# A pair of images moved in one DMA of 128 rows, in place of eight DMAs of sixteen

## The chip, the cores and the metric

One core of one Trainium2 chip runs the whole program. The metric is the time on the device in microseconds (us). A core has five engines with their own instruction streams: TensorE (PE), VectorE (DVE), ScalarE (ACT), GpSimd (POOL) and SyncE (SP). They meet at semaphores. DMAs are issued here from SP's and from ScalarE's stream, and all of them are carried out by the core's 16 DMA engines.

## The reference

Input x has the shape (32, 64, 56, 56) in float32. Two residual blocks follow each other, and each begins with a group norm of 32 groups, so of two channels each:

```
x = x + conv3x3(sign(gn(x)), sign(weight)) * scale            # 64 -> 64 channels, padding 1
r = relu(batchnorm(w_r @ gn(x) + b_r))                         # 64 -> 16 channels
ker = w_s @ r + b_s                                            # 16 -> 16 groups x 49 taps, per pixel
x = x + sum over the 7x7 taps of shifted gn(x) * ker           # an involution: the kernel differs by pixel
```

w_r and w_s are weight-normalised. The involution's 49 coefficients of a pixel are shared by the four channels of a group.

## The kernel before

Two images make a pair; there are 16 pairs. A pair fills 128 partitions: the 64 channels of one image and the 64 of the other, 56 x 56 values in each, so one partition's row is 12544 contiguous bytes, in SBUF as in DRAM. The tile xs holds three pairs (`xs[:, p % 3, :]`). The pair is loaded there, both residual blocks are added to it in place, and it is stored from there.

The first block is a convolution on TensorE (L512), added to xs by VectorE (L750). For the second block the normalised image is transposed by TensorE (L541), split into a high and a low half in float16 by ScalarE (`high`, L404) and VectorE (`low`, L783), and written to a scratch tensor in DRAM (`parts_out`, L270). From there SP reads it back as patches: two stacks of sixteen-row planes, `first_stack` (L287, eight DMAs) and `second_stack` (L295, two DMAs; ScalarE copies the rest of the second stack from the first, `copy_high`, L432). A pair has 7 slots of patches (E = 7) and each slot has 8 units, so 56 units. In a unit TensorE multiplies the patches by the span weights (L571), VectorE multiplies the result by relu's output (L792), GpSimd adds two halves (L365), and TensorE sums these for a slot (L589). The sums go to DRAM and come back rearranged (L424, L445, issued by ScalarE), are arranged (L454), transposed (L603) and added to xs (L804, `added`).

Each engine's order is written out by hand. While pair p runs through its 56 units, the preparation of pair p + 1 is put between them: row sums (L734) at units 0 to 3, convolution at units 11 to 17, transposes with their high and low halves at units 28 to 36, and the reduction with its relu (L552, L412) at units 37 and 38. The relu is copied to the partitions where VectorE needs it by sixteen small DMAs (`spread`, L305), which wait for it.

SP's order matters for this change. In slot s of pair p it issues the second stack of the next slot and the first stack of the one after that. Behind these it issues, in slot 2, the store of pair p - 1 (`store`, L262), once the last output of that pair is added; in slot 3, two parts of pair p + 1 and the load of pair p + 2 (`load`, L257), once pair p - 1 is stored; in slot 4, the other two parts and spread. SP works its list in order, so a wait or a DMA there stands in front of all the rest.

Both `load` and `store` go through ROWS16 (L23), a list of eight slices of sixteen partitions: 32 to 92 in steps of 4, 0 to 30 in steps of 2, 33 to 93 by 4, 96 to 126 by 2, 34 to 94 by 4, 1 to 31 by 2, 35 to 95 by 4, and 97 to 127 by 2. Each slice is one DMA of 16 rows x 12544 bytes, 196 KB. Readers wait for all eight: x_loaded and stored count 16 for each DMA, and XLOAD and STORE are 128.

Of the kernel before, what the change touches and what calls it, by code (L numbers as in the profile page):

```python
# [20 lines left out]
OTHER = [i ^ 1 for i in range(32)]  # L21
K, PAD = 7, 3
TAPS = K * K  # L23

ROWS16 = tuple(slice(*r) for i in range(2) for r in ((32 + 2 * i, 96, 4), (i, 32, 2), (33 + 2 * i, 96, 4), (96 + i, 128, 2)))

PY, PX = 4, 2
POS = PY * PX
# [36 lines left out]
P_N = P_CONV + 9 * C  # L65

FIRST_LOADS, LOADS, ZEROS = 16 * 2, 16 * 6, 4
XLOAD, STORE = 16 * 8, 16 * 8
FIRSTLOAD, SECONDLOAD = 16 * 8, 16 * 2
COPY = JY * 128  # L70
DWRITE = 16 * 2
# [36 lines left out]
def build(nc, x, consts, params, span, gb_all, out, pairs=PAIRS):  # L108
    xv = x.rearrange("(p b) c h w -> p (b c) (h w)", b=2)
    ov = out.rearrange("(p b) c h w -> p (b c) (h w)", b=2)  # L110
# [4 lines left out]
    with ExitStack() as ctx:  # L115
        def sb(name, shape, dt=F32):
            return ctx.enter_context(nc.sbuf_tensor(name, shape, dt))

        def sem(name):
            return ctx.enter_context(nc.semaphore(name))  # L120
# [6 lines left out]
        xs = sb("xs", [128, 3, HW])  # L127
# [44 lines left out]
        x_loaded = sem("x_loaded")  # L172
        stored = sem("stored")
# [79 lines left out]
        @block.sync  # L253
        def _(sp):
            def load(p):
                for rows in ROWS16:
                    sp.dma_start(xs[rows, p % 3, :], xv[p][rows]).then_inc(x_loaded, 16)  # L257

            def store(p):
                sp.wait_ge(out_added, 4 * (p + 1))  # L260
                for rows in ROWS16:
                    sp.dma_start(ov[p][rows], xs[rows, p % 3, :]).then_inc(stored, 16)  # L262

            def parts_out(p, k):

# [43 lines left out]
            sp.dma_start(t_par, params).then_inc(first_loaded, 16)  # L309
            sp.dma_start(mask[:], consts[:, C_M:C_N]).then_inc(first_loaded, 16)  # L310
            load(0)
            for dst, src in ((t_span, span), (t_gb, gb_all.broadcast_to((128, 2 * TAPS * GROUPS))),
                             (t_sel, consts[0:TAPS, C_SEL:C_E]), (ident[:], consts[:, C_ID:C_ID + 128]),
# [4 lines left out]
            if pairs > 1:  # L318
                load(1)
# [10 lines left out]
            for p in range(pairs):  # L330
                for s in range(E):
                    e = E * p + s
                    if e + 1 < EALL:
                        second_stack(e + 1)
                    if e + 2 < EALL:
                        first_stack(e + 2)
                    if p + 1 < pairs:
                        if s == 3:
                            parts_out(p + 1, 0)
                            parts_out(p + 1, 1)  # L340
                        if s == 4:
                            parts_out(p + 1, 2)
                            parts_out(p + 1, 3)
                            spread(p + 1)
                    if s == 2 and p > 0:
                        store(p - 1)
                    if s == 3 and p + 2 < pairs:
                        if p > 0:
                            sp.wait_ge(stored, STORE * p)
                        sp.wait_ge(x_loaded, XLOAD * (p + 2))  # L350
                        load(p + 2)
            store(pairs - 1)
            sp.wait_ge(stored, STORE * pairs)

# [560 lines left out]
```

## Time and profile before

| | |
|---|---|
| three timed runs | 1971.62 us median (1965.9 to 1975.86) |
| the profiled execution | 1978.51 us, span 1976.6 us |
| granted TensorE clock, mean | 0.922 |
| TensorE, busy | 1621.0 us, 82% |
| VectorE, busy | 1378.6 us, 70% |
| ScalarE, busy | 1052.8 us, 53% |
| GpSimd, busy | 1015.0 us, 51% |
| SP's DMA queue (q1) | 139728 packets, 356.81 MB, 74.2% of 16 engines' span |
| ScalarE's DMA queue (q10) | 75264 packets, 51.39 MB, 10.1% |

A row of the timeline names the start, the duration, the engine, the line of the program, the operation, the tile written and the tile read, and the count of instructions merged; in brackets stands how long the engine was idle before it and what ended that. SPq and ACTq are the streams that issue DMAs; the duration of such a row is the time of issuing, and the transfer itself lands later. A wait is put down to the releaser that came last.

### The profile page before, as it was taken

How to read it: one execution, taken by the hardware profiler on the slowest of the kernel's cores; microseconds unless marked ns; L12 is line 12 of the kernel's file. 1: busy time of each engine (PE TensorE's matmuls, PEld its weight loads, DVE VectorE, ACT ScalarE, POOL GpSimd, SP SyncE). 2: the span in 40 equal slices, each digit the busy share in tenths (PEclk: the TensorE clock that was granted, in tenths of full speed). 3: DMA queues.
4: the chain of work that ended last, by engine and by line, in shares of the span. 5: the costliest groups of instructions: out<-in, count | busy, mean ns of one | idle time of the engine just before them, and what ended most of it. 6: DMA issues, size and time to landing. Idle time of an engine off the chain costs nothing.

```text
span 1976.6 us, 39046 instructions
## 1 busy us (share of the span) xinstructions
PE 1621.0 (82%) x15072; PEld 730.2 (37%) x15072; DVE 1378.6 (70%) x1699; ACT 1052.8 (53%) x758; POOL 1015.0 (51%) x904
## 2 busy tenths in 40 slices
PE   3488897978889797896978878798887988889885
PEld 1233443434333343343433334333333433334332
DVE  5476776858768685776867767586776767768674
ACT  2255555545655554555545655465555545655562
POOL 1145555554645555455554645555455554645673
PEclk8799998999999998998989989898989999989997
DMA  4679899797998969899798998979799797998993
GB/s 106 158 168 237 185 238 224 199 233 172 245 216 217 236 173 239 186 244 215 188 240 181 250 215 205 230 183 247 175 240 225 187 250 180 248 215 205 227 243 85
DMA packets 215178, 410.70 MB, mean 208 GB/s; under 512 B 87406, under 2 KB 134815, under 8 KB 210847
## 3 DMA queue, kind: packets, MB, share of 16 engines
q1 hardware_dynamic: 139728, 356.81, 74.2%
q10 hardware_dynamic: 75264, 51.39, 10.1%
q8 instruction: 119, 1.95, 0.5%
q14 instruction: 67, 0.55, 0.1%
HBM read 310.30 MB, written 84.93 MB: 200 GB/s over the span
## 4 chain that ended last, share of the span: by engine, by line
POOL 46%; issue 42%; SPq 4%; DMA 2%; DVE 2%; PE 2%; ACT 1%; POOLq 1%; ACTq 0%; DVEq 0%
POOL folded L365 46%; SPq L305 2%; DMA patches<-parts_dram 1%; SPq L287 1%; PE ybank L571 1%; DMA back<-consts_dram 1%; POOLq L364 0%; SPq L257 0%; ACT patches L432 0%; DVE prod L792 0%; SPq L295 0%; PE ybank L541 0%; DMA parts_dram<-parts 0%; DVE parts L783 0%; SPq L270 0%
## 5 line engine op out<-in xcount | busy, mean ns | idle before, releaser
L365 POOL TENSOR_TENSOR folded<-prod 128x448 f32<-128x448 f32 x896 | 1009.3, 1139 | 941.3 <-DVE prod L792 940.0
L792 DVE TENSOR_TENSOR prod<-ybank,relu 128x896 f32<-128x896 f32 x896 | 961.1, 1088 | 406.9 <-PE ybank L571 333.4
L571 PE MATMUL ybank<-patches,wspan 128*64 128x448 f16 x7168 | 863.7, 382 | 240.2 <-DMA patches<-parts_dram 110.4
L432 ACT ACTIVATE patches<-patches 96x1792 f16<-96x1792 f16 x448 | 736.8, 1689 | 589.8 <-DMA patches<-parts_dram 306.9
L571 PEld LDWEIGHTS ybank<-patches,wspan 128*64 128x64 f16 x7168 | 396.3, 116 | 757.6 <-issue 416.1
L512 PE MATMUL ybank<-sgn,convw 128*128 128x448 bf16 x1008 | 205.6, 357 | 24.5 <-ACT sgn L385 20.1
L589 PE MATMUL obank<-folded,esum 128*32 128x448 f32 x1792 | 214.8, 551 | 1.5 <-POOL folded L365 1.5
L582 PE MATMUL obank<-patches,wbias 128*32 128x448 f16 x3584 | 197.8, 364 | 0.0
L512 PEld LDWEIGHTS ybank<-sgn,convw 128*128 128x128 bf16 x1008 | 93.4, 97 | 137.8 <-issue 33.5
L582 PEld LDWEIGHTS obank<-patches,wbias 128*32 128x32 f16 x3584 | 87.4, 99 | 105.2 <-issue 52.7
L783 DVE TENSOR_TENSOR parts<-ybank,parts 128x1024 f16<-128x1024 f32 x64 | 78.5, 1226 | 60.5 <-ACT parts L404 60.5
L750 DVE SCALAR_TENSOR_TENSOR xs<-ybank,scale,xs 128x896 f32<-128x896 f32 x64 | 66.0, 1032 | 73.7 <-PE ybank L512 73.6
L404 ACT ACTIVATE parts<-ybank 128x1024 f16<-128x1024 f32 x64 | 65.3, 1020 | 68.1 <-PE ybank L541 64.5
L603 PE MATMUL ybank<-back,blocks 128*128 128x128 f32 (+1 forms) x448 | 62.2, 284 | 44.2 <-DVE prod L792 36.0
L541 PE MATMUL ybank<-ident,xn 128*128 128x128 f32 x512 | 74.3, 293 | 20.9 <-DVE parts L783 20.1
L420 ACT ACTIVATE osb<-obank,alpha 128x448 f32<-128x448 f32 x112 | 69.3, 619 | 29.7 <-PE obank L589 29.7
L603 PEld LDWEIGHTS ybank<-back,blocks 128*128 128x128 f32 (+1 forms) x448 | 48.2, 153 | 77.7 <-DVE prod L792 52.2
L541 PEld LDWEIGHTS ybank<-ident,xn 128*128 128x128 f32 x512 | 59.4, 148 | 44.4 <-DVE parts L783 25.5
L454 ACT ACTIVATE blocks<-rows 128x1792 f32<-128x1792 f32 (+1 forms) x32 | 54.1, 1690 | 40.0 <-DMA relu<-blocks 31.9
L754 DVE BATCH_NORM_STATS2 bn<-xs 128x6 f32<-128x448 f32 x112 | 70.2, 627 | 3.9
L804 DVE TENSOR_TENSOR xs<-ybank,xs 128x1024 f32<-128x1024 f32 (+1 forms) x64 | 61.8, 966 | 12.8 <-PE ybank L603 12.7
L734 DVE TENSOR_REDUCE rowsums<-xs 128x14 f32<-128x784 f32 x64 | 61.1, 959 | 12.5 <-DMA xs<-x_dram 12.5
(90 smaller groups left out, 380.0 us busy)
## 6 DMA issues: line engine op xcount, KB each, us to landing
patches<-parts_dram SPq DMA_DIRECT2D x1120, 224.0 KB, 7.0
parts_dram<-parts SPq DMA_DIRECT2D x128, 256.0 KB, 7.7
xs<-x_dram SPq DMA_DIRECT2D x128, 196.0 KB, 5.0
sums_dram<-osb ACTq DMA_DIRECT2D x112, 224.0 KB, 6.2
rows<-sums_dram ACTq DMA_DIRECT2D x112, 224.0 KB, 6.6
out_dram<-xs SPq DMA_DIRECT2D x128, 196.0 KB, 3.7
relu<-blocks SPq DMA_DIRECT2D x256, 49.0 KB
patches<-gb_dram SPq DMA_DIRECT2D x1, 784.0 KB
```

The source lines that it names most:

```text
L365: pool.tensor_tensor(folded[:, u % 8, :], prod[:, u % 2, 0, :], prod[:, u % 2, 1, :], ALU.add).then_inc(fold_done, 1)
L420: act.activation(osb[:], Obank[e % 2][:, 0:N], ACT.Copy, scale=alpha[:]).then_inc(o_read, 1)
L432: act.activation(X2[0:COPIED_ROWS, e % 2, at], X1[0:COPIED_ROWS, e % 3, at], ACT.Copy).then_inc(copied, 1)
L512: mm = pe.matmul(bank("conv", p, k)[:, i, 0:CW], convw[:, tap, :], sgn[:, CR * row + dh:CR * row + dh + CR, dw:dw + W], start=(tap == 0), ...
L541: mm = pe.transpose(bank("t", p, k)[:, y, 128 * h:128 * h + 128], xn[:, COLS * cy:COLS * cy + COLS], ident[:])
L571: mm = pe.matmul(bank("unit", p, n)[64 * t:64 * t + 64, h, 0:N], wspan[:, stack, g, h, :], of_group(e, stack, g), start=(stack == 0), stop ...
L582: pe.matmul(Obank[e % 2][32 * t:32 * t + 32, 0:N], wbias[:, stack, g, :], of_group(e, stack, g), start=(stack == 0 and i == 0), stop=False)
L589: mm = pe.matmul(Obank[e % 2][32 * (gp // 2):32 * (gp // 2) + 32, 0:N], esum[:, 16 - 16 * (gp % 2):48 - 16 * (gp % 2)], folded[:, 4 * half ...
L603: mm = pe.transpose(bank("out", p, k)[:, i, rows * n:rows * (n + 1)], V[0:rows, by].rearrange("m b g c -> m (b g c)"), back[0:rows, group, ...
L754: link(dve.bn_stats(bn[:, row, :], at[:, i, :]))
L783: dve.tensor_tensor(at(1), bank("t", p, k)[:], at(0), ALU.subtract).then_inc(low_done, 1)
L792: dve.tensor_tensor(prod[:, u % 2].rearrange("m h (n c) -> m h n c", c=GC), bank("unit", p, n)[:, :, 0:N].rearrange("m h (n c) -> m h n c" ...
```

## The change

The load of a pair becomes one DMA over all 128 partitions, and so does the store. The list ROWS16 goes, and the counts that readers wait for fall from 16 x 8 to 16. Nothing else is touched: the order on SP, the tiles and the bytes moved are the same.

```
-ROWS16 = tuple(slice(*r) for i in range(2) for r in ((32 + 2 * i, 96, 4), (i, 32, 2), (33 + 2 * i, 96, 4), (96 + i, 128, 2)))
...
-XLOAD, STORE = 16 * 8, 16 * 8
+XLOAD, STORE = 16, 16
...
             def load(p):
-                for rows in ROWS16:
-                    sp.dma_start(xs[rows, p % 3, :], xv[p][rows]).then_inc(x_loaded, 16)
+                sp.dma_start(xs[:, p % 3, :], xv[p]).then_inc(x_loaded, 16)
 
             def store(p):
                 sp.wait_ge(out_added, 4 * (p + 1))
-                for rows in ROWS16:
-                    sp.dma_start(ov[p][rows], xs[rows, p % 3, :]).then_inc(stored, 16)
+                sp.dma_start(ov[p], xs[:, p % 3, :]).then_inc(stored, 16)
```

## Rows read from the trace of the kernel before

**Rows 1.** Waits of the engines: engine, line, waited for: us, times, longest.

```profile
PE ybank L571 <- DMA patches<-parts_dram: 110.4, 15, 9.1
...
ACT patches L432 <- DMA sums_dram<-osb: 68.3, 13, 7.4
...
PE ybank L541 <- DVE parts L783: 20.1, 10, 3.2
...
DVE scale L672 <- DMA back<-consts_dram: 5.6, 1, 5.6
```

**Rows 2.** Waits of SP's queue.

```profile
SPq L305 <- ACT blocks L412: 20.0, 9, 4.1
```

**Rows 3.** Timeline of SP's queue, one pair, 493 to 550 us.

```profile
493.85 5.97 SPq L262 DMA_DIRECT2D out_dram<-xs  x8
499.92 1.89 SPq L295 DMA_DIRECT2D patches<-parts_dram  x2
502.04 5.21 SPq L287 DMA_DIRECT2D patches<-parts_dram  x8
...
512.87 5.67 SPq L257 DMA_DIRECT2D xs<-x_dram  x8
...
525.24 2.79 SPq L270 DMA_DIRECT2D parts_dram<-parts  x4
529.05 13.36 SPq L305 DMA_DIRECT2D relu<-blocks  x16
```

**Rows 4.** Timeline of TensorE, the same pair.

```profile
496.93 0.95 PE L571 MATMUL ybank<-patches,wspan 128*64 128x448 f16 x8
...
519.83 1.09 PE L541 MATMUL ybank<-ident,xn 128*128 128x128 f32 x8 [2.09 <-DVE parts L783]
...
547.89 4.69 PE L571 MATMUL ybank<-patches,wspan 128*64 128x448 f16 x24 [8.33 <-DMA patches<-parts_dram]
```

**Rows 5.** Timeline of ScalarE, the same pair.

```profile
514.32 3.28 ACT L432 ACTIVATE patches<-patches 96x1792 f16<-96x1792 f16 x2 [4.01 <-DMA patches<-parts_dram]
517.51 1.00 ACT L404 ACTIVATE parts<-ybank 128x1024 f16<-128x1024 f32 x1
```

**Rows 6.** Stretches: engines' busy us, TensorE clock, DMA share, GB/s (last two).

```profile
4.00:11.50 7.50, 0.00 (x0) 0.00 (x0) 0.00 (x0) 1.35 (x2) 2.22 (x3) 1.00 0.98 214
11.90:13.30 1.40, 0.00 (x0) 0.00 (x0) 0.78 (x1) 0.00 (x0) 0.00 (x0) 1.00 0.97 383
...
518.60:529.00 10.40, 9.15 (x100) 3.24 (x104) 6.68 (x7) 6.77 (x6) 4.64 (x4) 1.00 1.01 220
```

**Rows 7.** DMA issues by line: count, size of one, median us to landing.

```profile
xs<-x_dram SPq DMA_DIRECT2D x128, 196.0 KB, 5.0
...
patches<-params_dram SPq DMA_DIRECT2D x1, 331.5 KB, 2.9
```

**Rows 8.** Timeline of SP's queue at the head.

```profile
0.73 0.40 SPq L309 DMA_DIRECT2D patches<-params_dram  x1
...
1.65 5.03 SPq L257 DMA_DIRECT2D xs<-x_dram  x8
...
12.51 4.93 SPq L257 DMA_DIRECT2D xs<-x_dram  x8
```

**Rows 9.** Timeline of ScalarE: relu's last piece in another pair.

```profile
883.03 1.07 ACT L412 ACTIVATE blocks<-ybank,red_bias,red_scale 128x784 f32<-128x784 f32 x1 [1.67 <-PE ybank L552]
```

**Rows 10.** Timeline of SP's queue: spread in three other pairs.

```profile
290.50 14.14 SPq L305 DMA_DIRECT2D relu<-blocks  x16
...
885.74 12.27 SPq L305 DMA_DIRECT2D relu<-blocks  x16
...
1825.62 2.83 SPq L270 DMA_DIRECT2D parts_dram<-parts  x4
1832.68 11.86 SPq L305 DMA_DIRECT2D relu<-blocks  x16
```

**Rows 11.** Timeline of SP's queue at the end.

```profile
1968.44 4.98 SPq L262 DMA_DIRECT2D out_dram<-xs  x8
```

## The prediction

> **What bounds the kernel now.** I read the waits first. Once in a pair TensorE stands still for a DMA of patches: 15 times, 110.4 us in all [rows 1]. The waits of SP's queue name ScalarE's relu 9 times, 20.0 us in all [rows 2]. Where these two stand to each other is seen in the timeline of SP for one pair [rows 3]: SP issues the store (eight pieces, 493.85), two and eight patch loads, writes of parts, the load of a later pair (eight pieces, 512.87), patch loads and writes again, then the sixteen small copies of spread (529.05 to 542.41), and only behind these the patch loads for which TensorE is waiting. It resumes at 547.89, after 8.33 us idle [rows 4]. So in this stretch SP's list and what the DMA engines have queued set the pace, and spread is the gate in it. What follows spread (patch loads, their landing, the resumption) is a chain of fixed length: what starts spread 1 us earlier ends the pair 1 us earlier.
>
> Spread waits for relu's second half on ScalarE: the 9 waits are these; in the other 6 pairs SP itself came last. Relu comes from the unit stream, in which TensorE has one stall of note between store and spread: the fourth transposes wait for VectorE's low half, 20.1 us in 10 times, the longest 3.2 [rows 1], 2.09 us at 519.83 in this pair [rows 4]. Behind it stands ScalarE's high half at 517.51, which ran only when two copies of patches ahead of it on ScalarE were done; those started at 514.32, 4.01 us late, for patch loads issued from 502.04 on behind the store [rows 5, 3]. So the store in front of these loads costs TensorE about 2 us in most pairs.
>
> **The rate of the two shapes.** At the head the pieces of sixteen rows run nearly alone: 214 GB/s with the engines 0.98 busy (4.00 to 11.50 us). Just behind them come setup loads, most of their bytes in 128 rows: 383 GB/s at 0.97 busy (11.90 to 13.30) [rows 6]. A piece of 196 KB lands 5.0 us after its issue in the median; the 331.5 KB of params, one transfer of 128 rows, 2.9 us after [rows 7]. So busy engines move 128-row loads 1.8 times as fast here. One pair is 128 x 12544 B = 1.61 MB: 7.5 us at 214 GB/s, 4.2 us at 383. A reservation: most bytes of the fast window are one source row read many times.
>
> A rule on this: the Trainium skill, SBUF — State Buffer, "Door 1: The DMA port swizzle", says that bandwidth goes with how many of 16 ports the partitions reach, and that partitions 0 to 31 reach eight. By it the four pieces with step 2 would go at half rate and the four with step 4 at its full 436 GB/s, where 1.61 MB take 3.7 us: an estimate of 1.85 + 3.7 = 5.5 us for the eight against 3.7, so 1.8 us saved per transfer in place of 3.3. The rows have the pieces slower than that, and I keep to the rows.
>
> **The change, part by part.** It removes 7 of 8 DMA issues in each of 16 loads and 16 stores, and adds no wait. Consumers waited for all eight pieces before, so nothing needs a part early.
>
> *SP's time.* Eight pieces take 5.03 us to issue; one 128-row load took 0.40 [rows 8]. Each load and store frees some 4.6 us of SP. Not all of it is worth something: behind the store the next patch loads also need the units of the slot before, whose last taps end at 496.93 + 0.95 = 497.88 [rows 4], and they were issued at 499.92 [rows 3]. They gain 2.0 us, not 4.6.
>
> *Relu earlier.* The store's bytes leave the engines about 2 us earlier too (see the tail), so the copies of 514.32 can start near 512.3, the high half near 515.5 and the fourth transposes about 2 us earlier. Over the run this stall is 20.1 us; I take 17, as each of the 10 waits may keep some 0.3 us. Bounds: 0 if the patch loads' own bytes set their landing, 20 if all goes.
>
> *SP late at spread.* In the 6 pairs without a recorded wait SP came last. In one, relu's last piece ended at 883.03 + 1.07 = 884.10 [rows 9] and spread began at 885.74 [rows 10], 1.64 us late. The load's 4.6 us take that lateness away. At half of this each, the six make 5 us; bounds 0 and 10. I take 4, since relu itself moves up.
>
> *Spread's own length.* Sixteen issues took 14.14 and 12.27 us in two of the pairs where SP's list ran on without a wait (so behind a full queue), 13.36 and 11.86 in two where SP had waited, since its writes of parts ended at 528.03 and 1828.45, before spread began [rows 3, 10]. The midpoints 13.2 and 12.6 differ by 0.6. With load and store each leaving the engines 3.3 us sooner (7.5 - 4.2), the queue at spread is shorter: 0.5 us in each of 15 pairs makes 8. Bounds: 0 (the pace is SP's own) and 15 x (13.2 - 11.86) = 20.
>
> *Head.* Load 0 is issued from 1.65, and SP sees it landed at 12.51 [rows 8], 10.9 us. One transfer: 0.4 issue, some 2.0 until the first bytes and for the receipt (params took 2.9 us, of which 331.5 KB at 383 GB/s are 0.9), 0.3 behind params, 4.2 data: 6.9, so 4.0 us earlier. The setup loads stand behind it on SP and move with it; VectorE waits for the last of them (5.6 us [rows 1]), so the head as a whole moves by about 4. Bounds: 1 (the rate of the pieces) and 5.
>
> *Tail.* The last store is issued from 1968.44 [rows 11] and the span ends at 1976.6: 8.2 us. One transfer: 0.4 + 2.0 + 4.2 = 6.6. I take 2 us; bounds -1 (0.4 + 2.0 + 7.5 = 9.9, less what of it the pieces had too) and 3.
>
> Cover: in steady state the load lands most of a pair ahead of its reader, so its own time costs nothing but queue; that cover stays.
>
> Sum: 17 + 4 + 8 + 4 + 2 = 35 us. The profiled execution took 1978.51 us (span 1976.6), above the highest of the three timed runs; 35 from it gives 1943.5. I carry the saving over to the median of the runs, 1971.62: 1936.6, and say 1936. What is late next: TensorE's 8 us stall behind spread stays whole, since units and spread move up together.
>
> **Rivals.**
>
> *Hidden anyway.* The patch loads fill the engines: 1.01 busy at 220 GB/s from 518.60 to 529.00 [rows 6]. If that queue is as long afterwards, only head and tail gain: 1971.6 - 6 = 1965.6. For it: the share. Against it: 110.4 us of stalls that end on a chain through SP, and the faster rate of 128-row loads. The Trainium skill, DMA: Bandwidth & Descriptors, "Issuing engines are not separate DMA queues", calls the sequencer's time for starting a DMA usually small against the DMA itself; by it SP's part of the sum (4 us, and much of the 17) would go, and this rival's time come. The rows differ: 5.03 us of issue stand against 4.2 to 7.5 us of data.
>
> *Not what it says.* The single transfer runs no faster than the pieces (the fast window is explained by its repeated source row). SP still gains its issues, and the patch loads come less than 2 us earlier: half of 17, the 4, head 1, tail 0: 13 to 14 us, 1958.
>
> *Slower.* A burst of 1.61 MB stands on all engines at once, and ScalarE's own transfers (sums out, rows in) share them. ScalarE waits for the sums before it goes on to copies (68.3 us in 13 waits [rows 1]). If each burst holds one such transfer up by its 4.2 us beyond what the pieces did, then copies, high half and relu come up to 4.2 us later, less the 2 gained, in 15 pairs: +33, less 6 at the ends: 1999. It decides from the point where that extra delay exceeds the 2 us that the patch loads gain. Against it: the pieces put the same bytes there, for longer.
>
> **How the numbers follow.** Forecast 0.62, not what it says 0.13, hidden 0.14, slower 0.11. The forecast's own range: all terms at their best bound would be 20 + 10 + 20 + 5 + 3 = 58, 1914, which is unlikely for all at once, so 1918; at half the sum, 1954. To leave out no more than 2 in 10 the range takes in 1958 and 1965.6: 1918 to 1967. A difference under 0.5% (10 us) is about what a measurement can't tell from none. Faster: the forecast nearly whole and most of the second case, 0.74; same: hidden and the rest, 0.16; slower 0.10.
>
> **What would show it.** Right: SP's store and load rows are x1 of about 0.4 us; copies of patches in this place wait 2 us or less behind the store, not 4; the transposes' wait for VectorE's parts falls from 20.1 towards 3; SP's wait for relu is recorded in nearly every pair and grows from 20.0 to above 60 us; spread is near 12 us; SP sees load 0 landed near 8.5 us, not 12.5; the end comes 6.6 us after the last store's issue. The 8 us stall stays. Wrong: the load's bytes still take over 7 us, or the same waits stand, or ScalarE's wait for sums doubles.

## The result and the profile after

The changed kernel took 1948.53 us in the median (1944.56 to 1952.72) where the kernel before took 1970.28 beside it: ratio 0.9888, 95% interval 0.9855 to 0.9922, so 15 to 29 us less. A second series gave 0.985 (0.9811 to 0.9889), 22 to 37 us less. The forecast was 35 us less, 1936. The profiled execution took 1947.81 us, its span is 1945.9.

The two shapes first. From 4 to 7 us the DMA engines move rows of load 0 alone, before and after; at the end only the last store is left, and the second stretch shown is in each kernel the time in which its bytes move. From the profile after (columns as in [rows 6], the last three are TensorE's clock, DMA share and GB/s):

```profile
4.00:7.00 3.00, 0.00 (x0) 0.00 (x0) 0.00 (x0) 1.26 (x2) 2.22 (x3) 1.00 0.96 389
1941.10:1945.10 4.00, 0.00 (x0) 0.00 (x0) 0.00 (x0) 0.00 (x0) 0.00 (x0) 0.50 0.96 401
```

The same two before:

```profile
4.00:7.00 3.00, 0.00 (x0) 0.00 (x0) 0.00 (x0) 1.35 (x2) 2.22 (x3) 1.00 1.00 243
1969.60:1975.80 6.20, 0.00 (x0) 0.00 (x0) 0.00 (x0) 0.00 (x0) 0.00 (x0) 0.50 0.81 259
```

Load 0 now moves at 389 GB/s where its pieces moved at 243. The last store's bytes pass in 4.0 us, at 401 GB/s, where they took 6.2 us, at 259; the engines were 0.81 busy there, and SP issued until 1973.42 [rows 11], so some of the 6.2 us may be the pace of its issues. In the median of all 16 stores, most of which run beside other transfers, the bytes pass in 4.6 us where they took 7.1 (from the first start to the last end of the trace's DMA records of 12544 bytes).

SP's queue after, at the head, in the pair that answers to [rows 3], and at the end:

```profile
1.66 0.43 SPq L254 DMA_DIRECT2D xs<-x_dram  x1
...
9.46 0.33 SPq L254 DMA_DIRECT2D xs<-x_dram  x1
...
484.91 0.34 SPq L258 DMA_DIRECT2D out_dram<-xs  x1
489.15 1.20 SPq L291 DMA_DIRECT2D patches<-parts_dram  x2
490.57 6.17 SPq L283 DMA_DIRECT2D patches<-parts_dram  x8
...
504.15 0.56 SPq L254 DMA_DIRECT2D xs<-x_dram  x1
...
511.81 2.55 SPq L266 DMA_DIRECT2D parts_dram<-parts  x4
518.21 13.08 SPq L301 DMA_DIRECT2D relu<-blocks  x16
531.39 1.26 SPq L291 DMA_DIRECT2D patches<-parts_dram  x2
...
1940.34 0.34 SPq L258 DMA_DIRECT2D out_dram<-xs  x1
```

An issue is one row of 0.3 to 0.6 us. SP sees load 0 landed at 9.46, not 12.51 [rows 8]. Behind the store SP now stands still for 3.9 us (485.25 to 489.15), until the units before are done, so of its saving there only 2 us are used (the next loads go out 4.2 us after the store's first issue, and 6.1 us before the change). Parts are out at 514.36 and spread begins at 518.21: SP waits 3.9 us for relu, where in this pair it waited 1.0 us before (528.03 to 529.05 [rows 3]). From the last issue to the end it is 5.6 us (1940.34 to 1945.9) against 8.2.

ScalarE and TensorE in the same pair (answering to [rows 5] and [rows 4]):

```profile
502.65 3.28 ACT L428 ACTIVATE patches<-patches 96x1792 f16<-96x1792 f16 x2 [1.09 <-DMA patches<-parts_dram]
506.00 1.02 ACT L400 ACTIVATE parts<-ybank 128x1024 f16<-128x1024 f32 x1
```

```profile
508.93 1.09 PE L537 MATMUL ybank<-ident,xn 128*128 128x128 f32 x8
...
536.11 4.32 PE L567 MATMUL ybank<-patches,wspan 128*64 128x448 f16 x22 [7.37 <-DMA patches<-parts_dram]
```

The copies start 502.65 - 484.91 = 17.7 us after the store's issue, where it was 20.5 (514.32 - 493.85 [rows 5, 3]); the fourth transposes at 508.93 wait no more; the stall behind spread stays. Over the run, from the waits and SP's waits after:

```profile
PE ybank L567 <- DMA patches<-parts_dram: 103.9, 15, 8.1
```

```profile
SPq L301 <- ACT blocks L408: 38.6, 15, 4.3
```

The transposes' wait for VectorE's parts was 20.1 us [rows 1]; on the page after, the idle time of that group is 1.0 us, of which 0.2 is this wait (column 2 behind the bar is idle time, then what ended most of it):

```profile
L537 PE MATMUL ybank<-ident,xn 128*128 128x128 f32 x512 | 71.0, 284 | 1.0 <-DVE parts L779 0.2
```

### The profile page after: what moved, and what is told of

The parts are those of the page before. It is cut to its first block, busy times and chain, and to the rows that moved or that the text cites. A ratio compares the mean times of both kernels' runs of the same rounds, so it can differ in the third digit from the quotient of the medians.

```text
span 1945.9 us, 38822 instructions
## 1 busy us (share of the span) xinstructions
PE 1615.7 (83%) x15072; PEld 730.2 (38%) x15072; DVE 1377.2 (71%) x1699; ACT 1054.9 (54%) x758; POOL 1016.5 (52%) x904
## 3 DMA queue, kind: packets, MB, share of 16 engines
q8 instruction: 119, 1.95, 0.5%
## 4 chain that ended last, share of the span: by engine, by line
POOL 49%; issue 42%; PE 2%; SPq 2%; DVE 2%; DMA 2%; ACT 1%; POOLq 1%; ACTq 0%; DVEq 0%
POOL folded L361 49%; SPq L301 1%; PE ybank L508 1%; POOLq L360 1%; SPq L283 0%; DMA patches<-parts_dram 0%; PE ybank L567 0%; DMA xs<-x_dram 0%; DVE rowsums L730 0%; DVE prod L788 0%; DMA parts_dram<-parts 0%; PE ybank L537 0%; PE ybank L548 0%; ACT patches L428 0%; ACT sgn L381 0%
## 5 line engine op out<-in xcount | busy, mean ns | idle before, releaser
L800 DVE TENSOR_TENSOR xs<-ybank,xs 128x1024 f32<-128x1024 f32 (+1 forms) x64 | 61.8, 966 | 12.1 <-PE ybank L599 12.0
L392 ACT ACTIVATE xn<-xs,small 128x1568 f32<-128x1568 f32 x32 | 58.9, 1897 | 17.1 <-DVE small L772 17.0
```

## The experiments

All ratios are to the kernel before, run beside each. The theory after the result was that the store in front of the patch loads makes the gain, by its issues and by its rate; the rivals are in the expectations.

**e1_store_only**: the store in one transfer, the load in eight.

```
-XLOAD, STORE = 16 * 8, 16 * 8
+XLOAD, STORE = 16 * 8, 16
...
-                for rows in ROWS16:
-                    sp.dma_start(ov[p][rows], xs[rows, p % 3, :]).then_inc(stored, 16)
+                sp.dma_start(ov[p], xs[:, p % 3, :]).then_inc(stored, 16)
```

> The store alone in one transfer, the load still in eight. My theory: the gain of the steady state comes from the store that stands in front of the patch loads. Then TensorE's wait of the fourth transposes for VectorE's parts goes from 20.1 us to under 3, the last store takes 2.6 us less, the head stays (load 0 seen at 12.5 us), and the time is 14 to 18 us below before, some three quarters of the whole change's 22. Rival, that both transfers matter alike because the DMA engines are full all through: about half, 8 to 11 us, and the transposes' wait stays above 8 us.

Measured: 1965.94 us, 0.9968 (0.9948 to 0.9988), 6 us less. The mechanism came, the time did not. The transposes' wait is gone, but SP is late:

```profile
PE ybank L540 <- DVE parts L782: 0.9, 2, 0.5
```

```profile
508.36 5.00 SPq L257 DMA_DIRECT2D xs<-x_dram  x8
...
520.08 2.54 SPq L269 DMA_DIRECT2D parts_dram<-parts  x4
522.72 14.56 SPq L304 DMA_DIRECT2D relu<-blocks  x16
```

Parts end at 522.62 and spread follows at 522.72 without a wait; SP recorded one wait for relu in the whole run, 3.7 us, against 9 before. From the store's issue to relu's end it is 33.3 us in the mean of the 14 pairs that have both a store and a spread (35.2 and 34.3 in the two profiles of the kernel before), and to spread's start 34.1 (35.5 and 34.7). So spread starts at the later of two paths, relu's and SP's list with the load in it, and 0.5 of the 1.5 us that relu gains in a pair is lost on the other. The 1.0 us that is left would make 14 us over the run. But from spread's start to the next store a pair takes some 0.7 us more than before (the last three rows of the table at the end of this section), and why it does stays open.

**e2_load_only**: the load in one transfer, the store in eight (the other half of the diff).

> The load alone in one transfer, the store still in eight. My theory: it saves 3 us at the head (load 0 seen at 9.5 and not 12.5 us) and SP's lateness at spread (some 4 us over the run; SP then waits for relu in all pairs), while the transposes' wait stays near 20 us: 5 to 8 us below before. Rival, both matter alike: 11 us or more and a smaller transposes' wait.

Measured: 1956.2 us, 0.9915 (0.9886 to 0.9944), 16 us less: more than the store, against my theory. The transposes still wait, and SP now waits for relu in all 15 pairs:

```profile
PE ybank L540 <- DVE parts L782: 16.7, 11, 2.9
```

```profile
SPq L304 <- ACT blocks L411: 54.3, 15, 5.2
```

So here relu's path is last, and SP's is free. In this profile (column e2 of the table at the end of this section) relu's path is as long as before, SP's lateness at spread of 0.3 us a pair is gone, spread takes 12.1 us where it took 12.6 and 12.8, and load 0 lands some 2 us earlier: 0.9 x 14 + 2 makes 15 us. But this profile is of the fastest of the six executions (1947.87 us), and the kernel after does not show so short a spread (12.6 and 12.3). The two halves multiply to 0.9968 x 0.9915 = 0.9883, the ratio of the whole.

**e3_eight_columns**: eight transfers each again, but of all partitions and an eighth of the row.

```
-                sp.dma_start(xs[:, p % 3, :], xv[p]).then_inc(x_loaded, 16)
+                for i in range(8):
+                    at = slice(i * HW // 8, (i + 1) * HW // 8)
+                    sp.dma_start(xs[:, p % 3, at], xv[p][:, at]).then_inc(x_loaded, 16)
...
(the store likewise)
```

> Load and store in eight transfers again, but each of all 128 partitions and an eighth of the row (1568 bytes), so SP's issuing time is that of before (about 5 us) and the shape on the DMA engines that of after. If SP's issuing time made the gain, the time is that of before (within 5 us) and the transposes still wait about 20 us. If the rate of the shape made it, the time is within 5 us of after, the transposes' wait is under 5 us, and a store's bytes pass in under 5.5 us where pieces of sixteen rows took 7. My guess is between: 60% of the gain, since the next patch loads are issued 2 us later than after, but stand behind fewer bytes.

Measured: 1949.26 us, 0.9882 (0.9857 to 0.9907): the whole gain, with eight issues kept; the guess of 60% was too low.

```profile
484.49 3.83 SPq L262 DMA_DIRECT2D out_dram<-xs  x8
488.73 1.20 SPq L295 DMA_DIRECT2D patches<-parts_dram  x2
...
504.46 3.93 SPq L256 DMA_DIRECT2D xs<-x_dram  x8
```

```profile
PE ybank L541 <- DVE parts L783: 2.8, 4, 1.7
```

SP spends 3.8 and 3.9 us on them, and behind the store its next loads go out at 488.73, 4.2 us after the store's first issue, as in the kernel after (489.15 - 484.91): this time was idle there anyway. The number of issues is not the cause. The last store's bytes pass nearly as fast as in one transfer:

```profile
1941.60:1946.00 4.40, 0.00 (x0) 0.00 (x0) 0.00 (x0) 0.00 (x0) 0.00 (x0) 0.50 1.00 365
```

Beside other transfers they do not: in the median of the stores they take 6.5 us (before 7.1, after 4.6), so that sign of the expectation, under 5.5 us, holds only at the end. And one part of SP's saving is kept here: the loads behind the store go out 4.6 us after its first issue in the mean of the pairs, where it was 6.0 before and 4.1 after.

**e4_two_halves**: two transfers, partitions 0 to 63 and 64 to 127.

```
+                for rows in (slice(0, 64), slice(64, 128)):
+                    sp.dma_start(xs[rows, p % 3, :], xv[p][rows]).then_inc(x_loaded, 16)
...
(the store likewise)
```

> Two transfers of 64 neighbouring partitions each: SP's issuing time is nearly that of after (0.7 us), the shape is another. By the Trainium skill, SBUF - State Buffer, Door 1, partitions 0 to 63 reach 8 of 16 ports, so each half would go at half rate and the load or store take an estimated 7.4 us of data. If the rate made the gain, the transposes' wait stays above 10 us and the time is 5 to 12 us below before; if SP's issuing time made it, the time is within 5 us of after and the wait under 3 us.

Measured: 1991.34 us, 1.0086 (1.0056 to 1.0115): 17 us slower than before, and some 40 slower than one transfer. The sign that the rate should give held, the transposes' wait; the time, expected 5 to 12 us below before, was missed on the slow side. SP's time is nearly as short as that of after (1.14 us for the last store, 0.34 there); the rate is not as high. The same two stretches:

```profile
4.00:7.00 3.00, 0.00 (x0) 0.00 (x0) 0.00 (x0) 1.44 (x2) 2.21 (x3) 1.00 0.97 230
1981.30:1988.70 7.40, 0.00 (x0) 0.00 (x0) 0.00 (x0) 0.00 (x0) 0.00 (x0) 0.50 0.95 215
```

```profile
PE ybank L539 <- DVE parts L781: 26.6, 14, 3.2
```

The engines are 0.95 to 0.97 busy at 215 to 230 GB/s where whole transfers move 389 to 401; the transposes' wait is above that of before. The last store's bytes take 7.4 us, as the expectation estimated, and more than in eight pieces (6.2). Behind a store the next loads go out 4.4 us after its first issue in the mean, nearly as early as after the change, and still relu's end comes 35.9 us after it (before 35.2 and 34.3): SP's time brings nothing at this rate. Fewer, larger transfers with little more than half the rate lose; the shape decides.

**e9_two_sixty_fours** measures the shape by itself: a first transfer of 64 rows, partitions 32 to 95 in even pairs, 0 to 63 in odd ones, then the rest in two.

```
+                if p % 2 == 0:
+                    sp.dma_start(ov[p][32:96], xs[32:96, p % 3, :]).then_inc(stored, 16)
+                    sp.dma_start(ov[p][0:32], xs[0:32, p % 3, :]).then_inc(stored, 16)
+                else:
+                    sp.dma_start(ov[p][0:64], xs[0:64, p % 3, :]).then_inc(stored, 16)
+                    sp.dma_start(ov[p][64:96], xs[64:96, p % 3, :]).then_inc(stored, 16)
+                sp.dma_start(ov[p][96:128], xs[96:128, p % 3, :]).then_inc(stored, 16)
...
(the load likewise)
```

> Three transfers per load and store; the first is 64 rows, of even pairs partitions 32 to 95, of odd pairs 0 to 63, so two transfers of the same size, place and number of descriptors that differ in their partitions alone. If the partitions reached set the rate (the Trainium skill, SBUF - State Buffer, Door 1: 32 to 95 reach 16 ports, 0 to 63 reach 8), the median landing of a store is near 3.5 us for 32 to 95 and near 5.5 us for 0 to 63 (802816 bytes: 1.9 us against 3.8 us of data at the two rates that the stores of the earlier runs showed). If the number of rows or of transfers sets it, the two land alike, within 0.5 us.

Measured, one line of the program at a time, partitions 32 to 95 and then 0 to 63 (us from issue to landing):

```profile
L265 SPq DMA_DIRECT2D out_dram<-xs x8: 594/594/617, 256.0 to 1894.9; - x8
...
DMA to landing us min/median/max: 3.8/3.9/7.5
```

```profile
L268 SPq DMA_DIRECT2D out_dram<-xs x8: 537/542/545, 372.1 to 1964.7; - x8
...
DMA to landing us min/median/max: 5.7/6.0/6.2
```

Same number of rows, same bytes, same place: 2.1 us apart. That agrees with the Trainium skill's "Door 1" (SBUF — State Buffer), by whose port map partitions 32 to 95 reach 16 ports and 0 to 63 reach 8. Here is its number: on the partitions that it gives half the ports, 0.80 MB take 2.1 us longer. For loads the medians differ by little, 6.7 against 7.1 us; that transfers ahead of them hide the difference is likely, but not shown. The whole kernel took 1975.89 us in its single run, about what the kernel before took beside it (1975.72).

**e10_neighbours**: the kernel before with eight pieces of sixteen neighbouring partitions.

```
-ROWS16 = tuple(slice(*r) for i in range(2) for r in ((32 + 2 * i, 96, 4), (i, 32, 2), (33 + 2 * i, 96, 4), (96 + i, 128, 2)))
+ROWS16 = tuple(slice(16 * i, 16 * i + 16) for i in range(8))
```

> The kernel before with its eight pieces of sixteen rows, but each of sixteen neighbouring partitions: the same number of issues, rows and bytes. If SP's issues or the size of a piece set the time, it is that of before, within 5 us. If the partitions of a piece do, a piece reaches 4 ports at most where it reached 8 or 16, a store's bytes take 12 us or more where they took 7, the last store's end comes 12 us or more after its issue, and the time is 40 us or more above before.

Measured: 2039.52 us, 1.0329 (1.0273 to 1.0385), 65 us slower with the same number of issues, rows and bytes. The direction holds; the size of one part was too large: the end comes 10.5 us after the last store's issue, not 12 (2030.88 to the span's end, 2041.4). SP's issuing got longer too, 6.9 us against 5.0 [rows 11], so not all of the 65 us need be the rate.

```profile
2030.88 6.88 SPq L262 DMA_DIRECT2D out_dram<-xs  x8
```

**e5_store_behind**: the kernel before, with the store moved behind the patch loads of the next slot.

```
-                    if s == 2 and p > 0:
-                        store(p - 1)
...
+                    if s == 3 and p > 0:
+                        store(p - 1)
                     if p + 1 < pairs:
                         if s == 3:
                             parts_out(p + 1, 0)
```

> The kernel before with all its pieces; only the store moves, from in front of the patch loads of the next slot to behind them. Theory after the first four runs: spread starts at the later of two paths, relu's (held up by the store's bytes in front of the patch loads) and SP's own list. Then relu comes at 33 us after the store's old place and not 35.2, the transposes' wait falls from 20.1 us to under 5, but SP's list is as long as before and SP now comes last at spread in nearly all pairs: 3 to 8 us below before. Rival, that the store's place is nothing and only its rate counts: within 3 us of before and the transposes' wait over 10 us.

Measured: 1996.93 us, 1.0119 (1.009 to 1.0149), 23 us slower. Neither theory held, and the experiment isn't clean: the store now stands in front of the writes of parts, and right behind it the load must wait for its landing.

```profile
PE ybank L541 <- DVE parts L783: 24.1, 13, 3.1
...
ACT parts L404 <- DMA parts_dram<-parts: 41.1, 15, 3.5
```

```profile
SPq L257 <- DMA out_dram<-xs: 20.5, 12, 2.8
```

ScalarE's high half now waits 41.1 us for those writes, where it waited 3.5 us before. It shows only that the store in pieces costs in this place too; its bytes, its issues and the load's wait behind it are not separated.

**e6_short_transfers**: the kernel after, nearly without the bytes.

```
+                if p < 3:
+                    sp.dma_start(xs[:, p % 3, :], xv[p]).then_inc(x_loaded, 16)
+                else:
+                    sp.dma_start(xs[0:16, p % 3, 0:16], xv[p][0:16, 0:16]).then_inc(x_loaded, 16)
...
+                if p == pairs - 1:
+                    sp.dma_start(ov[p], xs[:, p % 3, :]).then_inc(stored, 16)
+                else:
+                    sp.dma_start(ov[p][0:16, 0:16], xs[0:16, p % 3, 0:16]).then_inc(stored, 16)
```

> The kernel after, but from the fourth pair on a load moves only 16 rows of 64 bytes, and of the stores only the last moves all: the bytes of loads and stores are left out, the issues stay, most of the output is not written. Theory: after the change their bytes no longer set the pace, since relu's path is the units' own 33 us and spread is the gate; at most 6 us below after. Rival, that the DMA engines are full all through and every byte costs: 15 us or more below after.

Measured: 1929.61 us, 0.9796 (0.9756 to 0.9836): 13 to 19 us below the two medians of after, so nearer to the rival. The bytes still cost something after the change. Relu's path did not move (33.3 us in the mean, 33.1 after); spread did, 11.9 us in the mean of 14 against 12.6 and 12.3.

**e7_spread_shared**: the kernel after, with half of spread issued by ScalarE.

```
-                for t in range(2):
+                for t in range(1):
...
+            def spread_high(p):
+                act.wait_ge(r_done, 2 * (p + 1))
+                if p >= 2:
+                    act.wait_ge(prod_done, UNITS * (p - 1))
+                for dy in range(PY):
+                    for h in range(HALVES):
+                        act.dma_start(R[64 + 16 * dy:64 + 16 * dy + 16, p % 2, h, :],
...
                     if more and n in RED_AT:
                         relu(p + 1, RED_AT[n])
+                        if RED_AT[n] == 1:
+                            spread_high(p + 1)
```

> The kernel after, with eight of spread's sixteen DMAs issued by ScalarE right behind its relu, the other eight by SP as before. If spread's issuing on SP is the gate, as the prediction has it (1 us earlier ends the pair 1 us earlier), SP's row falls from 12.6 to 6.3 us, TensorE's stall behind it from 7.0 to about 1, and the time is 40 to 90 us below after. Rival, that what follows (the patch loads' bytes, or ScalarE's copies, later by ScalarE's eight issues) sets the pace: under 15 us below after, and the stall comes back one slot later.

Measured: 1914.43 us, 0.971 (0.9676 to 0.9743), 29 us below after run beside it, and the best of all. It lies between the two expectations.

```profile
509.44 6.81 SPq L301 DMA_DIRECT2D relu<-blocks  x8
516.35 2.93 SPq L291 DMA_DIRECT2D patches<-parts_dram  x2
```

```profile
528.75 4.60 PE L580 MATMUL ybank<-patches,wspan 128*64 128x448 f16 x24 [8.81 <-DMA patches<-parts_dram]
```

Spread is 6.3 us shorter, but the patch loads behind it, out at 516.35, let TensorE go on only at 528.75, 12.4 us later, where it was 536.11 - 531.39 = 4.7 us after the corresponding issue in the kernel after. In such pairs the patch loads land later instead; that they queue behind other bytes is the likely reason, not one that a run isolated. TensorE's waits for patches fell from 103.9 to 67.2 us, in 9 places.

**e8_after_again** and **e11_before_again** are second profiles of the two kernels.

> The changed kernel once more, with more runs and a second profile: 1945 to 1952 us, ratio 0.986 to 0.992. The second profile shows how far the parts of a pair differ between executions of one kernel: store to relu should again be 33.2 us in the mean, and spread 12 to 13.

> The kernel before once more, for a second profile: how far the parts of a pair differ between executions. Store to relu should again be 35 us in the mean and the transposes' wait near 20 us in 10 places; the stretch from TensorE's resumption to the next store may differ by 0.5 us a pair (some 7 us over the run).

Measured: 1943.08 us and 0.985 (0.9811 to 0.9889) for after; 1973.22 us, a single run, for before. Means over the 14 pairs, worked out from the rows of SP, ScalarE and TensorE (the last row over 13, as behind the last of them no pair is prepared); e1 and e2 stand beside them:

```
us                                 before   again   after   again      e1      e2
store's issue to relu's end         35.23   34.30   33.15   33.09   33.26   34.83
relu's end to spread's start         0.28    0.38    0.03    0.03    0.85    0.03
spread                              12.64   12.77   12.64   12.31   12.90   12.09
spread's end to TensorE's resuming   4.96    5.15    4.83    5.08    5.28    5.00
TensorE's resuming to next store    65.39   65.40   65.97   65.44   65.68   64.93
```

The first two rows differ between the kernels before and after by more than between executions of one; the others do not clearly. The transposes' wait in the second profile of before was 15.2 us in 13 places, so that the 20.1 of the first is an upper one.

## Why the prediction was right or wrong

The direction, the range and the gate (spread, and what starts it) hold: in the means of two profiles each, spread starts 1.95 us earlier in a pair and the pair is 2.0 us shorter. By its steps:

*Relu earlier*, taken as 17 us: from the table (35.23 + 34.30 - 33.15 - 33.09) / 2 = 1.65 us a pair, 23 us over 14. Right mechanism, a little small. The transposes' wait itself fell by what was taken for it, from 20.1 and 15.2 us to 0.2 and none recorded. So some 5 us of the 23 come from elsewhere on that path, and from where is not shown.

*SP late at spread*, 4 us: 0.3 us a pair, 4 us. Right. But the forecast added this to the former as if each came alone. e1 shows that they are two paths to one start: with the store alone relu gained nearly all of its time, and SP's lateness grew from 0.3 to 0.85 us a pair and took a third of it back.

*Spread's own length*, 8 us: mis-sized. It measured (12.64 + 12.77 - 12.64 - 12.31) / 2 = 0.23 us a pair, 3 us, and no more than executions differ by. That a queue lengthens it isn't refuted: without the bytes (e6) it is 11.9, with the slower pieces of e10 13.4. The term rested on 3.3 us off each transfer, which the rates do not bear out (below).

*Head*, 4 us: 12.51 - 9.46 = 3.05, and in the second profiles 11.89 - 10.05 = 1.84, so 2.4 in the mean. The rate was as taken, 389 GB/s against 383. But load 0's last row starts only at 8.38 us: the setup loads, issued behind it from 2.13 us on, move among its rows from about 7 us on. *Tail*, 2 us: 8.2 - 5.6 = 2.6.

These make 23 + 4 + 3 + 2.4 + 2.6 = 35 us; the spans of the profiles differ by 31 (1974.0 less 1943.2, means of two each), and the timed medians by 22 and 29. Some 4 us came back elsewhere; the stretch between TensorE's resuming and the next store lost 4 in the means (0.31 x 13), but differs by 7 between two executions of the kernel after (0.53 x 13), so where they came back stays open. That the parts add up to the forecast's 35 is luck in part: relu's term was 6 us too small and spread's 5 us too large. The forecast lies 6 to 13 us above the measured gain.

*The rate of the two shapes* was the step that mattered, and its reservation fell: 389 GB/s against 243 for the load, and 401 against 259 for the store, which has no repeated source row. What it saves was overrated. The forecast took 3.3 us off each transfer (7.5 - 4.2), with 214 GB/s from a stretch that runs on to 11.50 us and takes in setup loads [rows 6]. The last store shows 6.2 - 4.0 = 2.2 us and the median store 7.1 - 4.6 = 2.5 us, between those 3.3 and the 1.8 that the prediction set aside. In the steady state a whole load lands 9.7 us after its issue in the median, against 7.8 at the head (9.46 - 1.66); there patch loads stand beside it.

*SP's time*, 4.6 us per transfer, was right as a number, and is not the cause by itself. e3 keeps the eight issues and has the whole gain; e4 saves them and is slower than before. What no run separates is the 2 us by which the loads behind the store go out earlier: the runs in which the transposes' wait falls below 3 us (after, e1, e3, e6) have them, and no run has a store at the new rate with loads behind it as late as before. The rival "not what it says", by which the single transfer is no faster, is refuted by the rates, and e4 shows that its saved issues bring nothing at a lower rate; "hidden anyway" by the result, though e6 shows that bytes still cost 13 to 19 us; "slower" did not come: ScalarE's wait for sums went from 68.3 and 62.2 us to 75.5 and 70.4, 8 us in all 15 pairs together.

What would show it: SP's wait for relu was foretold above 60 us and is 38.6 (34.4 in the second profile), since the 4 us saved behind the store are spent there in a wait for units, and relu itself comes earlier.

## What to carry to other kernels

Before counting issues, look at GB/s in a stretch where one transfer has the DMA engines alone and busy: shapes with the same bytes differed by 1.5 to 1.9 times here (401 GB/s against 259 in strided pieces and 215 in halves), and that, not the number of DMAs, decided between gain and loss. Where a step starts at the later of two paths, an edit that shortens one shows its gain only up to the other, so measure each half by itself before adding them up. A gate that sits in one engine's list of issues can be worth as much as the transfers in front of it: giving half of spread to ScalarE's stream brought 29 us more.

## What the runs showed of the hardware that had not been expected

Which partitions a transfer covers set its time at the same number of rows: a store's 64 rows landed in 3.9 us from partitions 32 to 95 and in 6.0 from 0 to 63, and two halves of 64 moved at 215 to 230 GB/s with the engines 0.95 to 0.97 busy. Sixteen neighbouring partitions per piece lost less than I had expected: the last store's end came 10.5 us after its issue, against 8.2 for the strided pieces and 5.6 for one transfer.
